# A graph network on one core: VectorE's second operands in PSUM, and cell tables of 20 pairs of corners a node

## The reference

```
L0: twice  xw = einsum('ni,kio->nko', h, W)          # 25 matrices of 64x64
           g = xw[src[:, None], widx]; msg = einsum('es,eso->eo', basis, g)   # 4 corners of an edge's cell
           h = relu(segment_sum(msg, dst) / max(deg, 1) + h @ root + bias);  then cat([x, h1, h2]) @ final_w.T + final_b
L1: segment_sum(dinv[src] * dinv[dst] * x[src], dst)
L2: segment_sum(mlp([x[src], x[dst], e32]), dst), and a second mlp on [x, sum]
L3: three times  relu(segment_sum([x[dst], x[src], e16, 1] @ W.T + b, dst)), batch norm between them
```

## Time and profile before

| | us |
|---|---|
| median of 3 runs | 19718.14 (19655.34 to 19722.63) |
| the profiled execution, its own time | 19663.67 |
| its span, first to last instruction | 19661.8 |
| first gather of pass 0 starts at | 725.5 |
| last gather of pass 6 starts at | 19625.6 |

### The profile page before, as it was taken

The page is one execution under the profiler, slowest core; times in us unless marked ns, Lnnn a source line. Parts: engine busy times, 40 slices in busy tenths (PEclk is TensorE's granted clock), DMA queues, the critical chain, the costliest instruction groups (busy, mean ns, idle before and its releaser), DMA issues.

```text
span 19661.8 us, 145045 instructions
## 1 busy us (share of the span) xinstructions
PE 8407.5 (43%) x34014; PEld 7084.8 (36%) x34014; DVE 4924.1 (25%) x8122; ACT 1228.1 (6%) x2808; POOL 11671.0 (59%) x11663
## 2 busy tenths in 40 slices
PE   7655555444443333334444433333323333333333
PEld 4333334333333333334444433333323333233333
DVE  5334444333342111112333321111111111211111
ACT  3101111000000000001111100000000000000000
POOL 0366666577676666656555556566556665466665
PEclk9877777677775555556766755555555555555555
DMA  7545555333332111113333321111111111111111
GB/s 292 215 148 175 186 173 188 114 100 101 98 101 55 27 30 30 30 43 91 92 91 91 90 51 24 23 23 24 21 28 24 23 24 23 26 24 26 26 25 25
DMA packets 1013135, 1476.05 MB, mean 75 GB/s; under 512 B 546589, under 2 KB 704574, under 8 KB 987470
## 3 DMA queue, kind: packets, MB, share of 16 engines
q0 software_dynamic: 426240, 764.57, 15.9%
q1 hardware_dynamic: 586830, 710.77, 10.7%
HBM read 970.98 MB, written 503.39 MB: 75 GB/s over the span
## 4 chain that ended last, share of the span: by engine, by line
another core or an unknown queue 55%; PE 17%; issue 14%; DVE 6%; POOL 3%; DMA 2%; SPq 1%; ACT 1%; DVEq 1%; ACTq 0%; POOLq 0%
PE PS L769 10%; PE PS L689 4%; POOL BIG L612 3%; DVE OH L1356 1%; DVE BIG L1369 1%; PE PS L802 1%; DMA AG<-acc 1%; PE PS L698 1%; PE PS L763 1%; DVE BIG L1376 1%; DVE BIG L1195 0%; DVE BIG L1384 0%; PE PS L678 0%; ACT STG L971 0%
## 5 line engine op out<-in xcount | busy, mean ns | idle before, releaser
L769 PE MATMUL PS<-BIG,OH 128*128 128x64 f32 (+3 forms) x23310 | 5759.4, 428 | 4181.3 <-DVE OH L1356 1549.7
L612 POOL DMA_INDIRECT BIG<-t_mp,IDX x4995 | 4832.4, 967 | 3306.8 <-issue 1790.0
L769 PEld LDWEIGHTS PS<-BIG,OH 128*128 128x128 f32 x23310 | 5073.8, 295 | 4741.2 <-issue 2524.9
L612 POOL DMA_INDIRECT BIG<-t_cell,IDX x3330 | 3594.9, 1080 | 2504.7 <-issue 1814.5
L1356 DVE TENSOR_TENSOR OH<-REL,IOTA 128x640 f32<-128x640 f32 x2331 | 1899.8, 822 | 3262.8 <-remote 2640.3
L763 PE MATMUL PS<-STG,CARRY 128*128 128x64 f32 (+3 forms) x1554 | 552.2, 452 | 4690.2 <-ACT STG L971 2899.5
L612 POOL DMA_INDIRECT BIG<-t_p,IDX x1665 | 1623.2, 975 | 1167.2 <-issue 478.5
L612 POOL DMA_INDIRECT BIG<-t_gcn,IDX x1665 | 1619.3, 973 | 976.1 <-issue 559.1
L763 PEld LDWEIGHTS PS<-STG,CARRY 128*128 128x128 f32 x1554 | 344.0, 276 | 4877.8 <-ACT STG L971 2868.2
L1369 DVE TENSOR_TENSOR BIG<-BIG,COEF 128x1280 f32<-128x1280 f32 x666 | 990.4, 1487 | 553.6 <-DMA BIG<-t_cell,IDX 520.4
L802 PE MATMUL PS<-BIG 128*128 128x128 f32 x3330 | 584.8, 338 | 995.9 <-DVE BIG L1376 822.1
(11 more groups left out here) (148 smaller groups left out, 3336.0 us busy)
## 6 DMA issues: line engine op xcount, KB each, us to landing
t_cell<-BIG SPq DMA_DIRECT2D x198, 2048.0 KB, 6.3
BIG<-in_dst_row SPq DMA_DIRECT2D x333, 240.0 KB
BIG<-t_mp,IDX POOLq DMA_INDIRECT x4995
BIG<-t_cell,IDX POOLq DMA_INDIRECT x3330
BIG<-t_gcn,IDX POOLq DMA_INDIRECT x1665
BIG<-t_p,IDX POOLq DMA_INDIRECT x1665
BIG<-in_ef SPq DMA_DIRECT2D x333, 80.0 KB
BIG<-t_q SPq DMA_DIRECT2D x333, 48.0 KB
```

The costliest lines, as they stand in the source:

```text
L612: nc.gpsimd.indirect_dma_start(to[:, j, :], None, table, bass.IndirectOffsetOnAxis(ap=IDX[:, s // CHUNKS, at:at + 1], axis=0)).then_inc(ga ...
L769: last = nc.tensor.matmul(WIN[:, 0:out_w], OH[:, s % CHUNKS, j * P:(j + 1) * P], src[:, j, :], start=False, stop=(s % CHUNKS == CHUNKS - 1 ...
```

## The change

Two edits. First, second operands of DVE: `IOTA` is copied once into PSUM (`PIOTA`, bank 1), and `OH` and `CARRY` are compared with that copy. The weights of a group are copied by DVE from `COEF` into PSUM (`PCOEF`, bank 1, 128x60), one group ahead of their use, and the product reads them there. SP reloads `COEF` behind that copy (`coef_copied`) instead of behind the products. The PSUM tiles `HIDP`, `RF`, `YB` and one transpose target move to other banks, so that bank 1 holds nothing else.

Second, the cell tables: for each node 20 pairs of corners of 128 floats, in the order 5*u + v, in place of 16 cells of 256. A cell is two pairs that follow each other, so a gather still reads 256 floats, at a multiple of 128. The copies of a block fall from eight to five (ACT 3, DVE 2, each 128x512), its store from 2 MB to 1.31 MB, and the second table's buffers rise from two to three.

```diff
-CELLS = 16
-CELL_W = 4 * F
+PAIRS = 20
+PAIR_W = 2 * F
+CELL_W = 2 * PAIR_W
...
+        PIOTA = bank(1, P)
+        PCOEF = [PS[:, 512 + P + gi * TILES * 4:512 + P + (gi + 1) * TILES * 4] for gi in range(UNIT)]
...
-        def halves(ph, b, v):
-            cells = cell_buffer(ph, b).rearrange("p (v u c) -> p v u c", v=4, u=4)
-            upper = [cells[:, v - 1, :, 2 * F:4 * F]] if v > 0 else []
-            lower = [cells[:, v, :, 0:2 * F]] if v < 4 else []
-            return upper + lower
+        def pairs_of(ph, b, v):
+            return cell_buffer(ph, b).rearrange("p (u v c) -> p v u c", u=4, v=5)[:, v, :, :]
...
                             if kind == "spline":
-                                sp.wait_ge(prod_ready, CHUNKS * (gb + g))
+                                sp.wait_ge(coef_copied, gb + g)
...
-                    for half in halves(ph, b, v):
-                        nc.scalar.activation(half, corner_pairs(v), copy).then_inc(sem(f"{ph}_xw_act"), 1)
+                    nc.scalar.activation(pairs_of(ph, b, v), corner_pairs(v), copy).then_inc(sem(f"{ph}_xw_act"), 1)
...
-                    for half in halves(ph, b, q):
-                        v.tensor_copy(half, corner_pairs(q)).then_inc(sem(f"{ph}_xw_dve"), 1)
+                    v.tensor_copy(pairs_of(ph, b, q), corner_pairs(q)).then_inc(sem(f"{ph}_xw_dve"), 1)
...
-                        v.tensor_scalar(CARRY[:, :], IOTA[:, :], DELTA[:, bass.ds(g, 1)], None, ALU.is_equal
+                        v.tensor_scalar(CARRY[:, :], PIOTA, DELTA[:, bass.ds(g, 1)], None, ALU.is_equal
...
-                                    IOTA[:, :].unsqueeze(1).to_broadcast(shape), ALU.is_equal).then_inc(oh_ready, 1)
+                                    PIOTA.unsqueeze(1).to_broadcast(shape), ALU.is_equal).then_inc(oh_ready, 1)
+                def copy_coefficients(gi, u):
+                    dve.wait_ge(coef_in[gi], 16 * (ub + u + 1))
+                    v.tensor_copy(PCOEF[gi], COEF[:, gi, :]).then_inc(coef_copied, 1)
...
+                        if s % CHUNKS == 0 and not (last and gi == UNIT - 1):
+                            copy_coefficients((gi + 1) % UNIT, u if gi < UNIT - 1 else u + 1)
...
-                        dve.wait_ge(coef_in[gi], 16 * (ub + u + 1))
+                        dve.wait_ge(coef_copied, gb + u * UNIT + gi + 1)
...
-                        w = COEF[:, gi, s % CHUNKS * CT * 4:(s % CHUNKS + 1) * CT * 4]
+                        w = PCOEF[gi][:, s % CHUNKS * CT * 4:(s % CHUNKS + 1) * CT * 4]
```

More of the change, by code:

```diff
@@ L81, in sem @@
             return named[name]
-        t_cell = [dram(f"t_cell{l}", (z.rows * CELLS, CELL_W)) for l in range(2)]
+        t_cell = [dram(f"t_cell{l}", (z.rows * PAIRS, PAIR_W)) for l in range(2)]
         t_gcn = dram("t_gcn", (z.rows, F))
@@ L162, in gnn_program @@
         SLOT_W = CT * SUM0_W
-        XW_W = CELLS * CELL_W
+        XW_W = PAIRS * PAIR_W
         g_end = SLOTS * SLOT_W
-        BIG = sb("BIG", [P, g_end + 2 * XW_W])
+        big_end = g_end + max(3 * XW_W, z.blocks * F + 2 * F)
+        BIG = sb("BIG", [P, big_end])
         DSTF = BIG[:, SLOT_W:SLOT_W + z.tiles]
@@ L168, in gnn_program @@
         SLOTI = BIG[:, SLOT_W + 2 * z.tiles:SLOT_W + 3 * z.tiles].bitcast(I32)
-        big_end = g_end + 2 * XW_W
         COEFT = BIG[:, big_end - 4 * z.tiles:big_end]
@@ L172, in gnn_program @@
         XW = {"n0": [BIG[:, big_end - (3 - n) * XW_W:big_end - (2 - n) * XW_W] for n in range(3)],
-              "n1": [BIG[:, big_end - (2 - n) * XW_W:big_end - (1 - n) * XW_W] for n in range(2)]}
+              "n1": [BIG[:, big_end - (3 - n) * XW_W:big_end - (2 - n) * XW_W] for n in range(3)]}
         D = BIG[:, big_end - z.blocks * F - 2 * F:big_end - 2 * F].rearrange("p (b f) -> p b f", f=F)
@@ L200, in gnn_program @@
         WIN, ROW = bank(0, SUM0_W), bank(6, P)
-        HIDP = bank(1, CT * HID)
-        TB = {"n0": 2, "n1": 2, "n2": 2, "n3": 2, "n4": 5, "n5": 2, "n6": 2, "n7": 2}
-        RF = bank(1, NB * 2 * F)
+        PIOTA = bank(1, P)
+        PCOEF = [PS[:, 512 + P + gi * TILES * 4:512 + P + (gi + 1) * TILES * 4] for gi in range(UNIT)]
+        HIDP = bank(2, CT * HID)
+        TB = {"n0": 2, "n1": 4, "n2": 2, "n3": 2, "n4": 5, "n5": 2, "n6": 2, "n7": 2}
+        RF = bank(6, NB * 2 * F)
         FB = bank(4, NB * F)
@@ L207, in gnn_program @@
         AGG = bank(6, NB * F)
-        YB = bank(3, NB * F)
+        YB = bank(4, NB * F)
         UB = bank(7, NB * P)
@@ L227, in gnn_program @@
         carry_ready, win_staged, sums_landed = sem("carry_ready"), sem("win_staged"), sem("sums_landed")
-        ea_copied = sem("ea_copied")
+        ea_copied, coef_copied = sem("ea_copied"), sem("coef_copied")
         gathered = [sem(f"gathered{s}") for s in range(SLOTS)]
@@ L351, in _ @@
             loads[0] = 16 * len(todo)
-            for ph, n in (("n0", 3), ("n1", 2)):
+            for ph, n in (("n0", 3), ("n1", 3)):
                 for b in range(n):
@@ L384, in store_cells @@
             def store_cells(ph, k, b):
-                sp.wait_ge(sem(f"{ph}_xw_act"), 4 * (k * NB + b + 1) + 4)
+                sp.wait_ge(sem(f"{ph}_xw_act"), 3 * (k * NB + b + 1) + 3)
                 hold(sp)
-                sp.wait_ge(sem(f"{ph}_xw_dve"), 4 * (k * NB + b + 1) + 4)
+                sp.wait_ge(sem(f"{ph}_xw_dve"), 2 * (k * NB + b + 1) + 2)
                 hold(sp)
-                rows = t_cell[int(ph[1:])].rearrange("(n p u) c -> n p (u c)", p=P, u=CELLS)
+                rows = t_cell[int(ph[1:])].rearrange("(n p u) c -> n p (u c)", p=P, u=PAIRS)
                 n = len(XW[ph])
@@ L686, in cells @@
                 for v in range(5):
-                    copied = sem(f"{ph}_xw_dve" if v % 2 else f"{ph}_xw_act")
-                    pe.wait_ge(copied, 4 * (k * NB + b) + (1, 2, 3, 4, 4)[v])
+                    if v % 2:
+                        pe.wait_ge(sem(f"{ph}_xw_dve"), 2 * (k * NB + b) + v // 2 + 1)
+                    else:
+                        pe.wait_ge(sem(f"{ph}_xw_act"), 3 * (k * NB + b) + v // 2 + 1)
                     nc.tensor.matmul(bank(CELL0 + v, 5 * F), HT[0:F, b * P:(b + 1) * P],
@@ L709, in node_slot @@
                         products(sem(f"{ph}_rf_ps"), [HT[0:F + 1, :]], [RFW[n][:, :]], 2 * F,
-                                 lambda b: 512 + b * 2 * F)
+                                 lambda b: 6 * 512 + b * 2 * F)
                     if s == 4:
@@ L742, in node_slot @@
                         pe.wait_ge(sem("n4_u_ready"), k + 1)
-                        products(sem("n4_y_ps"), [UT[:, :]], [UW2[:, :]], F, lambda b: 3 * 512 + b * F)
+                        products(sem("n4_y_ps"), [UT[:, :]], [UW2[:, :]], F, lambda b: 4 * 512 + b * F)
                 if n >= 4:
@@ L886, in _ @@
             for ph in ("n0", "n1"):
-                act.sem_inc(sem(f"{ph}_xw_act"), 4)
+                act.sem_inc(sem(f"{ph}_xw_act"), 3)
             act.sem_inc(win_staged, 1)
@@ L1082, in _ @@
             for ph in ("n0", "n1"):
-                dve.sem_inc(sem(f"{ph}_xw_dve"), 4)
+                dve.sem_inc(sem(f"{ph}_xw_dve"), 2)
             dve.sem_inc(sem("sums_used"), 1)
@@ L1088, in _ @@
             link(v.tensor_scalar(MASK[:, :], MASK[:, :], float(z.nodes), None, ALU.is_lt))
+            link(v.tensor_copy(PIOTA, IOTA[:, :]))
             link(v.tensor_scalar(IDENT[:, :], IOTA[:, :], PIDX[:, 0:1], None, ALU.is_equal))
@@ L1145, in _ @@
             e2 = ev.rearrange("p (t d) -> p t d", d=2)
-            link(v.scalar_tensor_tensor(out=flat, in0=f2[:, :, 1], scalar=4.0, in1=f2[:, :, 0],
+            link(v.scalar_tensor_tensor(out=flat, in0=f2[:, :, 0], scalar=5.0, in1=f2[:, :, 1],
                                         op0=ALU.mult, op1=ALU.add))
             link(v.tensor_copy(SLOTF, SLOTI))
-            link(v.scalar_tensor_tensor(out=flat, in0=SLOTF, scalar=float(CELLS), in1=flat,
+            link(v.scalar_tensor_tensor(out=flat, in0=SLOTF, scalar=float(PAIRS), in1=flat,
                                         op0=ALU.mult, op1=ALU.add))
@@ L1396, in fast_pass @@
                     add_rows(z.units - 1, SLOTS - 1)
+                elif kind == "spline":
+                    copy_coefficients(0, 0)
+                    edged_units(dve, body, node)
                 else:
```

## The result

The change made the kernel slower: 20151.59 us (median of 3, 20148.19 to 20154.05) against 19718.14, a ratio of 1.0232 [1.0203, 1.0261]. The forecast was 19600, with a range of 19230 to 19880.

A forecast was written before the change was run, and what follows sets the result against it. POOL's issue of gathers sets each pass's floor, with stretched gathers and stops for index lists on top. Terms 12 + 108 + 0 = 120 us off 19663.7 give 19544; with 54.5 for the median, 19600 us, range 19230 to 19880.

The forecast's parts named there:

- The second operands on DVE: DVE's one-hots, products and CARRY cost 0 more with PSUM operands; new weight copies 44 to 152 us, taken as 0.
- The stretch goes: POOL's gathers, slowed while DVE reads two SBUF operands, lose that extra time: 666 us at most, bar part of pass 3's.
- So I count the stretch of pass 1 as exchanged for stops: 0 gained; likewise pass 0's, and the 215 us of passes 2 to 6: On POOL, gather time freed returns as waits for index lists, one for one, judged by passes 1 and 2: 0 gained.
- Stops take more than the stretch gives: Rival: without breaks POOL waits longer for its lists, up to +231 us, 19949, or about 19880 in part; chance 0.22.
- The stretch is worth its whole price: Rival: POOL's freed gather time shortens the passes, 18950 us in full, 19275 at half; chance 0.22 for half or more.
- the cells' 120: Gain from cheaper cell-table making: 12 us ahead of pass 0 plus 108 in pass 0.
- SP's wait: SP's reload of weights waits for their copy instead of the products; the window store stands ahead anyway: 0 gained.
- Cells ahead of pass 0: Making the first cell table is bound by PE's products, so shorter stores and fewer copies gain only 12 us.
- Cells in pass 0: Fewer DVE copies ahead of the awaited list (82 us) and shorter stores (26) take 108 us off pass 0.
- Signs: Forecast wrong if pass 1 falls below 2450 or rises over 2640 us, or the prologue shrinks by more than 40.

The follow-up runs named there:

- e10: The kernel before the change, unchanged, measured against itself on a chip with late signals: 19641.14 us, 1.0008 of before.
- e9: The changed kernel measured once more, against the kernel before on a chip with late signals: 19857.94 us, 1.0124.
- e11: The kernel of e3 (tables of pairs and moved banks only) repeated against the kernel before, late signals: 19493.13 us, 0.9915.
- e3: The changed kernel with IOTA and weights both read from SBUF again, leaving pairs and moved banks, against the kernel before: 19728.32 us, 1.0023.
- e1: The changed kernel with one-hots and CARRY reading IOTA from SBUF again, weights still in PSUM, against the kernel before: 19843.99 us, 1.0075.
- e2: The changed kernel with weights read from SBUF, no copy, SP's old wait, IOTA still in PSUM, against the kernel before: 19979.55 us, 1.0151.
- e4: The changed kernel plus a 128x512 iota on POOL behind each chunk's five gathers, against the kernel before, late signals: 19825.99 us, 1.0061.
- f4: The changed kernel with list load ahead of window store and a 128x512 iota on POOL per chunk, against the kernel before: 19005.97 us, 0.9688.
- g2: Pairs alone (both operands in SBUF) with list load ahead of window store, against the kernel before, prompt signals: 16406.03 us, 0.9980.
- e8: The kernel before with SP's list load moved ahead of the window store, against the kernel before, prompt signals: 16423.58 us, 0.9986.
- f2: The kernel before with SP's list load moved ahead of the window store, against the kernel before, late signals: 18938.64 us, 0.9651.
- f3: Pairs alone (both operands in SBUF) with list load ahead of window store, against the kernel before, late signals: 18812.18 us, 0.9579.
- e12: The changed kernel with SP's list load moved ahead of the window store, against the kernel before, late signals: 19006.16 us, 0.9688.
- g1: The changed kernel measured against the kernel before on a chip with prompt signals: 15832.20 us, 0.9633.

## Why the prediction was wrong, point by point

**The second operands on DVE: right, but for a small part.** Product and one-hot cost nothing more, the copies 48 us (222 x 0.217) of hidden time; `CARRY` at 57 ns more was priced at 0, hidden as well. The rule of the Trainium skill cited there ("VectorE: DVE Perf Modes", "The TRN2 errata") has the trace against it for the two large forms (816 against 822 ns, 1481 against 1487), while the 57 ns of `CARRY` are near the estimated 65 worked out from the rule's cycles.

**The stretch goes: right.** Its 666 us fell to 16. The inference in "SBUF — State Buffer", "Who interferes with whom", of the Trainium skill, that descriptor generation isn't held up, does not hold for these gathers, since they became faster when DVE's second operand left SBUF (1085 to 947 ns on average in pass 1). The rule above it in that list, on a GpSimd instruction that reads SBUF, agrees with the trace; whether it is the reading of the indices that waits no run separates.

**"So I count the stretch of pass 1 as exchanged for stops: 0 gained; likewise pass 0's, and the 215 us of passes 2 to 6": this step failed.** The rate of one for one was read from two passes with different work, pass 1 and pass 2. The runs put 1128 us of new stops in place of 650 of stretch, 1.7 to 1, in the first measurement, and 731 in place of 604, 1.2 to 1, between the profiled executions of e10 and e9. Both hold the pairs' gain as well; without it, it was 1.5 to 1 (e11 to e9), 1.4 to 1 for the products of passes 0 and 1 (e3 to e1) and 2.2 to 1 for the one-hots of passes 2 to 6 (e3 to e2). So the direction was right and the term, put at 0, was mis-sized: its two sides differ by 478 us in the first measurement. By pass the stops of the first measurement grew by 304, 340, 110, 170, 58, 63 and 85 us. The mechanism of the rival "Stops take more than the stretch gives" is the one that came: passes 0 and 1 fell into the cycle of two lists and a stop. The rival's size was too small, 231 us for a measured 433. It put pass 1 at 2690 (measured 2663) and pass 6 at 2631 (2620), passes 0 and 3 lower than they came (2690 for 2808; 2741, unchanged, for 2867). What the rival held against itself, that the others don't need more time for the same work, was the mistake: the others did take longer for the same work once the breaks were gone. That they get their signals through in the breaks is the likely reason and is argued, not shown. e4 and f4 show that a break costs nothing, but the updates of `chunk_done` that come over 1 us late don't come mainly in breaks: in the kernel before 3.6 of them come in 100 us of stretched gathers (over 1.2 us) and 3.3 in 100 us of undisturbed ones, and only the stops have more, 6.4; in e4's pauses it is 5.4, in f4's 3.1.

That the chips differ was beyond the trace of one execution. With prompt signals the rival "The stretch is worth its whole price" is the right one: 604 us off, where it gave 766 with the cells' 120, which aren't there on such chips (g2 against e8: 0.998 and 0.999).

**SP's wait: 0, not told apart.** e2 brings it back with the weights in SBUF; I did not try it by itself.

**Cells ahead of pass 0: PE-bound, right.** The first gather starts at 724.4, 1 us earlier than before and not 200: shorter stores give nothing here. Of the 12 us taken 1 came.

**Cells in pass 0, -108: near, but unsteady.** With the operands in SBUF pass 0 went from 2813 us to 2689 (e10 and e11, one chip) and from 2780 to 2689 (f2 and f3, one chip), -124 and -91. In e3 it was 2768. With the operands in PSUM the changed kernel had pass 0 at 2808 in the first measurement, 90 above; this gain was covered by new stops. The kernel before is itself unsteady here, 2718 us in the earlier trace rows and 2813 in e10, as much apart as the whole gain.

**Signs.** I had named a pass 1 over 2640 as what would make me wrong; it came to 2663. Its length less POOL's busy time, 746 in the earlier trace rows, became 1086: up by 340 for 230 of stretch.

## What is open

Why signals are late on some chips is not settled; no run changes it by itself. With the list first, 1880 us of e12's stops are waits for `chunk_done`; how far the other 1600, for lists, are late signals of gathers' landing, of the copies of weights or of the lists' own landing isn't told apart. Why removing a stretch of POOL's gathers costs more in stops than it frees, by a rate from 1.2 to 2.2, is not shown. Nor did a run with late signals tell the loss of breaks from a cost of the PSUM operand itself; with prompt signals that operand costs nothing (g1's passes). e3 and e11, the same kernel, differ by 1.1% in ratio, so chips with late signals aren't all alike.

## What to carry to other kernels

Idle gaps on the engine that bounds a kernel can be doing work: before removing a slowdown, look at what the other engines do in that time, and test it by adding a pause of known length and seeing whether the time moves. An exchange rate between a loss and a wait should be measured by undoing the change one part at a time on one chip, and not read from two stages with different work; the pause shows whether there is an exchange at all. Put the load that the bounding engine waits for ahead, in its queue's order, of stores that depend on other engines; and measure a small change on several chips, always beside the kernel before.

## What the runs showed of the hardware that was not expected

The same program takes 19.6 to 19.7 ms on some chips and 16.44 ms on others, each with a spread under 1%, with the same durations of undisturbed gathers (944 and 945 ns at median) and of products (1487 and 1490 ns on average). The difference is in signals and sequencers while POOL streams gathers. SP's lines for the list load of the changed kernel, first with late signals, then with prompt ones (ns min/median/max; the registers' arithmetic and the issue of a list):

```profile
L466 SPq FUSED_REGOPS  x735: 2/51/1409, 819.6 to 20064.0; - x184
L466 SPq DMA_DIRECT2D IDX<-in_src x555: 2/351/1425, 6354.6 to 20092.0; - x185
```

```profile
L466 SPq FUSED_REGOPS  x735: 46/51/71, 787.9 to 15727.1; - x184
L466 SPq DMA_DIRECT2D IDX<-in_src x555: 327/343/722, 5069.1 to 15745.2; - x185
```

A register operation that takes 51 ns takes up to 1409 on the one and at most 71 on the other. Of SP's register and semaphore operations 2757 of 16162 took over 300 ns after the change (2620 of 16041 before), and none with prompt signals. After the change 36% of those that began while POOL streamed took over 300 ns (2539 of 7112), and 2.4% of those in its stops of over 3 us (203 of 8337). With prompt signals (e8) the update of `chunk_done` follows its matmul by 0.01 us at median and 0.02 at most. In pass 1 of the kernel before, the next recorded update follows by some 7 us on average and up to 56; there the trace has 2046 updates for 2331 chunks, so some of this can be records that are missing.
